# Attention and LoRA block on one core: FFN and next layer norm placed inside attention windows, split weights kept in memory, one distance table

## What is computed

```
x = x + attention(layernorm(x))
    q, k, v = x Wq^T, x Wk^T, x Wv^T ; q, k = rmsnorm(q) wq, rmsnorm(k) wk
    scores  = q k^T / sqrt(128) + slope[head] * (key position - query position), masked above the diagonal
    out     = softmax(scores) v ; y = out Wo^T
x = x + 2 * sum over experts h of (x_n A_h^T) B_h^T * 8 * softmax(x_n Wr^T + br)_h,   x_n = layernorm(x)
```

## Time and profile before

| | |
|---|---|
| Median of 3 runs | 2248.26 us (2247.36 to 2248.58) |
| The profiled execution, its own time | 2247.54 us |
| Span of the profile, first to last instruction | 2245.7 us |
| Busy: PE / DVE / ACT / POOL | 2168.2 / 1399.3 / 1185.8 / 912.5 us |
| Granted TensorE clock, mean | 0.993 of 2.4 GHz |
| DMA | 53.04 MB |

### The profile page before, as it was taken

The page is one execution under the profiler, slowest core; times in us unless marked ns, Lnnn a source line. Parts: engine busy times, 40 slices in busy tenths (PEclk is TensorE's granted clock), DMA queues, the critical chain, the costliest instruction groups (busy, mean ns, idle before and its releaser), DMA issues.

```text
span 2245.7 us, 33802 instructions
## 1 busy us (share of the span) xinstructions
PE 2168.2 (97%) x12540; PEld 1872.5 (83%) x12540; DVE 1399.3 (62%) x3492; ACT 1185.8 (53%) x3397; POOL 912.5 (41%) x912
## 2 busy tenths in 40 slices
PE   5999999999999999999869999999999999999997
PEld 5888888888888888888658888888888888888885
DVE  4666666566666666666656566665666666566666
ACT  3555555565555556555235555554555555455552
POOL 2444343444344444434124444434344344444441
PEclk9999999999999999999989999999999999999999
DMA  3001010010101001010120010100001010010001
GB/s 114 28 1 48 1 48 1 1 47 1 48 1 48 1 1 48 1 48 1 42 63 19 1 48 1 48 1 26 23 1 48 1 48 1 16 33 1 1 1 38
DMA packets 27907, 53.04 MB, mean 24 GB/s; under 512 B 3032, under 2 KB 3032, under 8 KB 27744
## 3 DMA queue, kind: packets, MB, share of 16 engines
q1 hardware_dynamic: 26112, 50.34, 7.0%
q10 hardware_dynamic: 1632, 0.55, 0.1%
HBM read 46.68 MB, written 4.19 MB: 23 GB/s over the span
## 4 chain that ended last, share of the span: by engine, by line
PE 93%; DVE 3%; ACT 1%; issue 1%; DMA 1%; POOL 1%; ACTq 0%
PE s_ps L863 25%; PE turn_ps L855 18%; PE o_ps L863 18%; PE q_ps L863 16%; PE y_ps L863 16%; DVE pT_lo L688 1%; DMA bias<-in_L_ffn_B 1%; ACT pT_hi L488 1%; DVE y L837 0%; ACT qn L531 0%; PE q_ps L1013 0%; DVE probs L716 0%; DVE stats L795 0%; DVE y L791 0%; POOL q_inv_t L583 0%
## 5 line engine op out<-in xcount | busy, mean ns | idle before, releaser
L612 POOL TENSOR_TENSOR probs<-probs,p_inv_t 128x896 f32<-128x896 f32 (+7 forms) x512 | 576.8, 1147 | 636.3 <-DVE p_inv_t L756 636.3
L488 ACT ACTIVATE pT_hi<-turn_ps 128x512 fp32r<-128x512 f32 x576 | 332.9, 600 | 485.6 <-PE turn_ps L855 483.6
L688 DVE TENSOR_TENSOR pT_lo<-turn_ps,pT_hi 128x512 fp32r<-128x512 f32 x576 | 383.0, 684 | 141.9 <-ACT pT_hi L488 138.6
L748 DVE CUSTOM_DVE_ANT_0 probs<-s_ps,bias 128x896 f32<-128x896 f32 (+7 forms) x512 | 381.3, 753 | 111.9 <-issue 110.4
L525 ACT ACTIVATE probs<-probs,neg_max 128x896 f32<-128x896 f32 (+7 forms) x512 | 396.1, 775 | 84.8 <-DVE neg_max L748 84.6
L855 PE MATMUL turn_ps<-ident,probs 128*128 128x128 f32 x2560 | 363.8, 278 | 23.8 <-POOL probs L612 9.5
L855 PEld LDWEIGHTS turn_ps<-ident,probs 128*128 128x128 f32 x2560 | 308.6, 143 | 77.0 <-POOL probs L612 15.4
L863 PE MATMUL s_ps<-kT_hi,qT_hi 128*128 128x512 f32 (+3 forms) x768 | 276.8, 360 | 0.3 <-DVE qT_lo L690 0.3
L863 PE MATMUL s_ps<-kT_hi,qT_lo 128*128 128x512 f32 (+3 forms) x768 | 262.8, 342 | 0.0
L863 PE MATMUL o_ps<-pT_hi,v_hi 128*128 128x512 f32 x576 | 249.4, 433 | 13.6 <-DVE pT_lo L688 13.2
L863 PE MATMUL s_ps<-kT_lo,qT_hi 128*128 128x512 f32 (+3 forms) x768 | 261.8, 341 | 0.0
(11 more groups left out here) (98 smaller groups left out, 3932.8 us busy)
## 6 DMA issues: line engine op xcount, KB each, us to landing
wq_raw<-in_L_attn_Wq SPq DMA_DIRECT2D x16, 1024.0 KB, 7.7
wo_raw<-in_L_attn_Wo SPq DMA_DIRECT2D x16, 1024.0 KB, 5.4
y<-in_L_attn_x SPq DMA_DIRECT2D x16, 256.0 KB, 3.2
wkv_raw<-in_L_attn_Wk SPq DMA_DIRECT2D x16, 256.0 KB, 2.8
wkv_raw<-in_L_attn_Wv SPq DMA_DIRECT2D x16, 256.0 KB, 3.0
out<-y SPq DMA_DIRECT2D x16, 256.0 KB, 2.0
bias<-in_L_ffn_A ACTq DMA_DIRECT2D x1, 256.0 KB
bias<-in_L_ffn_B ACTq DMA_DIRECT2D x1, 256.0 KB
```

Of the source, the lines that this page charges most:

```text
L488: nc.scalar.activation(target, source, ACT.Copy).then_inc(sems["hi_done"], 1)
L612: nc.gpsimd.tensor_tensor(row, row, p_inv_t[:, s % 2, h:h + 1].to_broadcast((P, L)), ALU.mult).then_inc(sems["p_ready"], 1)
L688: nc.vector.tensor_tensor(target, source, high.bitcast(F32), ALU.subtract).then_inc(sems["lo_done"], 1)
L748: nc.vector.tensor_tensor_reduce(out=probs[:, s % 2, h, 0:L], in0=s_ps[:, at_col:at_col + L], in1=bias[:, h, S - L:S], scale=-1.0, scalar= ...
```

## The change

The plans are written anew: PROLOGUE, GROUP_A (head groups of batch one, seven times), BOUNDARY (last group of batch one), FIRST_B, GROUP_B (six times), LAST. In place of counted offsets, each step has a number, and `after(engine, kind, ...)` waits for it. What is done otherwise:

- The layer norm of batch two, with its x turns, is in BOUNDARY. Its x is loaded into `wq_raw` and `wo_raw`, which no weight needs any more. The FFN of batch one runs in BOUNDARY (tiles 0 to 5) and FIRST_B (6 and 7), that of batch two in LAST. It has buffers of its own (two tiles deep), its logits go into a bank of the turn ring and are copied out by DVE, and its output uses `y_ps`.
- The FFN weights are loaded in BOUNDARY, into `wkv_raw`.
- After splitting a weight in batch one, SP writes both halves to DRAM (`keep_*`); in batch two it reads them back (`back_*`), and their turns and splits are gone.
- The bias tables are gone. q is divided by the head's slope through its norm, `score_max` adds the plain distance `rel` and scales by the slope.

```diff
-GROUP_PLAN = (
...
-    "inv_k turn.p.7.7 q_part.9.0 high.p.7.7 table.1 low.p.7.6 values.7.5 low.p.7.7 norm_k q_part.9.1 values.7.6 "
...
+BOUNDARY = (
...
+    "values.7.4 f_max.5 high.p.7.5 turn.p.7.6 f_exp.5 low.p.7.5 turn.p.7.7 high.p.7.6 f_inv.5 kv.3 f_gate.5 "
...
+    plans = {-1: read(PROLOGUE), NG - 1: read(BOUNDARY), NG: read(FIRST_B), LAST_W: read(LAST)}
+    group_a, group_b = read(GROUP_A), read(GROUP_B)
+    for w in range(LAST_W):
+        plans.setdefault(w, group_a if w < NG else group_b)
...
-        bias = sb("bias", [P, G, S])
+        f_x = sb("f_x", [P, 2, DM])
+        f_logits = sb("f_logits", [P, 2, P + NE])
...
+        def x_source(b, t):
+            if b == 0:
+                return y[:, t, :]
+            return wq_raw[:, t, :] if t < G else wo_raw[:, t - G, :]
...
+        wo_kept = nc.dram_tensor("wo_kept", [NG, 2, P, G * DM], F32).ap()
...
+            def keep_wo(w):
+                after(sp, "low", "wo", w, G - 1)
+                sp.dma_start(wo_kept[w, 0], woT_hi[:].rearrange("p c n -> p (c n)").bitcast(F32)).then_inc(wo_spilled, 16)
+                sp.dma_start(wo_kept[w, 1], woT_lo[:].rearrange("p c n -> p (c n)").bitcast(F32)).then_inc(wo_spilled, 16)
...
+            def back_wo(w):
+                g = w - NG
+                after(sp, "y", w - 1, NT - 1)
+                sp.wait_ge(wo_spilled, 32 * NG)
+                sp.dma_start(woT_hi[:].rearrange("p c n -> p (c n)").bitcast(F32), wo_kept[g, 0]).then_inc(wo_back, 16)
+                sp.dma_start(woT_lo[:].rearrange("p c n -> p (c n)").bitcast(F32), wo_kept[g, 1]).then_inc(wo_back, 16)
...
+            def square_q(w, n):
...
+                    last = nc.scalar.activation(qn[:, h, :], q_ps[:, h * HD:(h + 1) * HD], ACT.Square,
+                                                scale=float(slopes[gg % NG * G + h]), accum_out=q_sum[:, h:h + 1])
...
-                    def table(h):
...
-                        nc.gpsimd.tensor_tensor(bias[:, h, :], rel[:],
-                                                slope_row[:, bass.ds(g * G + h, 1)].to_broadcast((P, S)),
-                                                ALU.mult).then_inc(sems["bias_ready"], 1)
...
+            def score_max(w, s, h):
...
+                nc.vector.tensor_tensor_reduce(
+                    out=probs[:, s % 2, h, 0:L], in0=s_ps[:, at_col:at_col + L], in1=rel[:, S - L:S],
+                    scale=-float(slopes[w % NG * G + h]), scalar=BIG, op0=ALU.add, op1=ALU.min,
...
+                elif of == "logits":
+                    t, = which
+                    after(pe, "low", "f", ffn_batch(w), t)
+                    for c in range(C):
+                        last = nc.tensor.matmul(bank[:, 0:P + NE], f_x[:, t % 2, c * P:(c + 1) * P], arT[:, c, :],
```

More of the change, by code:

```diff
@@ L273, in piece, with follow @@
+    number, counted = {}, {}
+    for w in range(-1, LAST_W + 1):
+        for item in plans[w]:
+            if item[0] == "q" and item[2] < C - 1:
+                continue
+            counted[item[0]] = counted.get(item[0], 0) + 1
+            number[named(w, *item)] = counted[item[0]]
+    def follow(work):
+        for w in range(-1, LAST_W + 1):
+            for kind, *what in plans[w]:
+                if kind in work:
+                    work[kind](w, *what)
     def piece(s, j):
@@ L281, in scores_col @@
         return 512 * (h % 2) if L <= 512 else 512 - min(512, L - 256)
-    def follow(work, plan):
-        for kind, *what in plan:
-            if kind in work:
-                work[kind](*what)
     with ExitStack() as ctx:
@@ new lines, in load_wq, with load_wo @@
+            def load_wq(w, *first):
+                g = 0 if first else w + 2
+                if g < NG:
+                    if not first:
+                        after(sp, "turn", "wq", g - 1, C - 1)
+                    sp.dma_start(wq_raw[:], wq_v[g]).then_inc(wq_loaded, 16)
+            def load_wo(w, *first):
+                g = 0 if first else w + 1
+                if g < NG:
+                    if not first:
+                        after(sp, "turn", "wo", g - 1, G - 1)
+                    sp.dma_start(wo_raw[:], wo_v[g]).then_inc(wo_loaded, 16)
@@ new lines, in high, with exp @@
+                    nc.scalar.activation(target, bank, ACT.Copy, scale=scale).then_inc(sems["high"], 1)
+            def exp(w, s, h):
+                after(act, "max", w, s, h)
+                row = probs[:, s % 2, h, 0:(s + 1) * P]
+                nc.scalar.activation(row, row, ACT.Exp, bias=neg_max[:, s % 2, h:h + 1], scale=-1.0,
+                                     accum_out=p_sum[:, s % 2, h:h + 1]).then_inc(sems["exp"], 1)
+            def square_q(w, n):
+                gg, s = w + n // NT, n % NT
+                if w < 0 and s == 0:
+                    act.wait_ge(small_loaded, 48)
+                after(act, "q", gg, s, C - 1)
+                for h in range(G):
+                    last = nc.scalar.activation(qn[:, h, :], q_ps[:, h * HD:(h + 1) * HD], ACT.Square,
+                                                scale=float(slopes[gg % NG * G + h]), accum_out=q_sum[:, h:h + 1])
+                last.then_inc(sems["square_q"], 1)
@@ new lines, in square_k, with v_high @@
+            def square_k(w, i):
+                after(act, "kv", w + 1, i)
+                for t in range(2):
+                    last = nc.scalar.activation(k_norm[:, 2 * i + t, :], s_ps[:, 512 * (i % 2) + t * 2 * HD:][:, 0:HD],
+                                                ACT.Square, accum_out=k_sum[:, 2 * i + t:2 * i + t + 1])
+                last.then_inc(sems["square_k"], 1)
+            def v_high(w):
+                after(act, "copy_kv", w + 1, C - 1)
+                if w >= 0:
+                    after(act, "values", w, NT - 1, NT - 1)
+                nc.scalar.activation(v_hi[:], kv_raw[:, :, HD:2 * HD], ACT.Copy).then_inc(sems["v_high"], 1)
@@ new lines, in o_high, with f_exp @@
+            def o_high(w, s):
+                after(act, "values", w, s, s)
+                nc.scalar.activation(oT_hi[:].rearrange("p h n -> p (h n)"), o_ps[:], ACT.Copy).then_inc(sems["o_high"], 1)
+            def f_exp(w, t):
+                after(act, "f_max", ffn_batch(w), t)
+                nc.scalar.activation(f_weights[:, t % 2, :], f_biased[:, t % 2, :], ACT.Exp, bias=f_neg_max[:, t:t + 1],
+                                     scale=-1.0, accum_out=f_sum[:, t:t + 1]).then_inc(sems["f_exp"], 1)
@@ L565, in _, with sort_b @@
+            def sort_b(w):
+                act.wait_ge(b_loaded, 16)
+                after(act, "turn", "wr")
+                nc.scalar.activation(b_sorted.rearrange("p o h r -> p h o r"), b_raw, ACT.Copy).then_inc(sems["sort_b"], 1)
+            follow({"high": high, "exp": exp, "square_q": square_q, "square_k": square_k, "v_high": v_high,
+                    "o_high": o_high, "f_exp": f_exp, "sort_b": sort_b})
         @block.gpsimd
@@ new lines, in normalise @@
+            def normalise(w, s, h):
+                L = (s + 1) * P
+                if h % 2 == 0:
+                    after(pool, "invert", w, s, h // 2)
+                row = probs[:, s % 2, h, 0:L]
+                nc.gpsimd.tensor_tensor(row, row, p_inv[:, s % 2, h:h + 1].to_broadcast((P, L)),
+                                        ALU.mult).then_inc(sems["normalise"], 1)
+            follow({"inv_q": inv_q, "inv_k": inv_k, "x_rstd": x_rstd, "f_rstd": f_rstd, "normalise": normalise})
@@ new lines, in add_f @@
+            def add_f(w, t):
+                after(dve, "f_out", ffn_batch(w), t)
+                nc.vector.tensor_tensor(y[:, t, :], y_ps[:], y[:, t, :], ALU.add).then_inc(sems["add_f"], 1)
+            follow({"x_stats": x_stats, "x_moments": x_moments, "x_norm": x_norm, "low": low, "max": score_max, "invert": invert,
+                    "norm_q": norm_q, "copy_kv": copy_kv, "norm_k": norm_k, "v_low": v_low, "o_low": o_low, "add_y": add_y,
+                    "f_stats": f_stats, "f_moments": f_moments, "f_norm": f_norm, "f_max": f_max, "f_inv": f_inv,
+                    "f_gate": f_gate, "f_low": f_low, "add_f": add_f})
@@ L846, in _ @@
         @block.tensor
         def _(pe):
[L848 to L857 removed]
+            pe.wait_ge(ident_ready, 1)
@@ new lines, in scores @@
+            def scores(w, s, h):
+                L = (s + 1) * P
+                if h == 0:
+                    if s == 0:
+                        after(pe, "low", "k", w, 1)
+                    after(pe, "low", "q", w, s)
+                n = s * G + h - (1 if L > 512 else 2)
+                if n >= 0:
+                    after(pe, "max", w, n // G, n % G)
+                col = scores_col(s, h)
+                edge = L if L <= 512 else 512 - col
+                for c, width in ((0, edge), (edge, L - edge)):
+                    if width == 0:
+                        continue
+                    last = split_product(s_ps[:, col + c:col + c + width],
```

(52 more changed lines are left out.)

933 lines of the change are left out of this document (403 added, 530 removed), and 338 rows, old and new, of tables (BOUNDARY, FIRST_B, GROUP_A, GROUP_B).

## The result

The changed kernel takes **2194.25 us** (median of 3 runs, 2194.18 to 2194.96) against 2248.26: ratio 0.976, interval 0.974 to 0.978. The forecast was 2159, range 2138 to 2190. The direction was right; the gain was 54 us where 89 were forecast, and the time lies 4 us above the range. The profiled execution's span is 2193.1 us.

The account below looks back on a forecast made before the run. PE, 97% busy, was taken to bound the kernel. Savings of 11.3 + 3.5 + 42.7 + 22.0 + 0.3 + 9.3 = 89.1 us took 2247.54 to 2158.4, forecast as a median of 2159, range 2138 to 2190.

Parts of the forecast that it names:

- The reloads: Kept weight halves read back in batch two: landing in 8.3 to 10.8 us, 3.6 to 6 to spare, cost 0.
- about as much room: Wq's reload between q.7.3 and q.8.0 was said to have about the slack of woT's, 3.6 to 6 us.
- The waits for k: New PE stall at scores.0.0, each window's end, for kT_lo: 0.9 us in batch one, 1.9 in batch two.
- w7: Batch one's last window, taking the next layer norm and six FFN tiles: 150.1 against 192.81 us, so -42.7.
- PE's own work in a steady window is 131.76 less 1.49 = 130.3 us.: Middle windows: window time less the 1.49 us spot where a probability piece is turned and at once needed.
- Same operations, other order: Batch one's windows before its last: reordering itself given no cost, only one stall going and another coming.
- the small waits: PE's minor waits beside the one for k: 0.3 us allowed per middle window of batch two.
- w9 to w14: Batch two's middle windows, ten turns fewer, bare k stall: 128.1 against 131.77 us each, -22.0 for six.
- FFN tile of 1.95 ... logits 0.47 ... the logits' row is two tiles: PE's price per FFN tile: turn 0.44, logits 0.47, gate turn 0.16, output 0.88; six tiles 11.7 us.
- w0 to w6: Batch one's windows before its last: 1.49 stall goes, 0.9 k stall comes, net -0.5 us each, -3.5 together.
- Rival 1: FFN-laden windows don't fit DVE (2174 us), or norms held by GpSimd's normalises at 0.95 each (2179); chance 0.20 for both.
- w15 and the end: Last window with six FFN tiles 127.5 us, then a 12.7 us tail: 140.2 against 149.46, so -9.3.

Follow-up runs that it names:

- the two corrected kernels: Changed kernel with k turned ahead of y.7, plus kv.3 ahead of values.7.4: 2172.2 us; plus q 9.3 behind values.7.7 as well: 2166.2 us.
- the fastest kernel: Changed kernel with k turned ahead of y.7, kv.3 earlier, q 9.3 behind values.7.7, GpSimd's normalises held behind the FFN's gates, PE's start waits filled: 2161.1 us.

## Why the prediction was right and wrong

**Right.** *The reloads*: no product waits for kept weights in the changed kernel; the halves of Wo land 4.9 and 7.0 us after their issue, where I had 8.3 to 10.8.

```profile
woT_hi<-wo_kept SPq DMA_DIRECT2D x8, 1024.0 KB, 4.9
woT_lo<-wo_kept SPq DMA_DIRECT2D x8, 1024.0 KB, 7.0
```

The step "about as much room" for Wq holds only since q 8.0 was moved too: the run that turned Wo in batch one's order shows what it costs otherwise. The waits for k were sized right, 0.85 for 0.9 and 1.94 for 1.9. norm_k takes 1.23 in all 16 groups. *w7* is right in its total, 151.69 against 150.1, but in part by luck: its work was set 3.2 too low (1.0 and 2.2, below) and its waits 2.3 too high; 0.7 of the miss stays unexplained.

**Wrong: "PE's own work in a steady window is 131.76 less 1.49 = 130.3 us."** This is the step that failed: it carried 16 windows. The 1.49 from 327.88 to 329.37 is a stretch of the chain, that is, ACT and DVE at work on the high and low half; it is not time in which PE stood. Up to 328.57 PE ran six score products:

```profile
327.62 0.37 PE L863 MATMUL s_ps<-kT_hi,qT_hi 128*128 128x256 f32 x1
...
328.29 0.28 PE L863 MATMUL s_ps<-kT_hi,qT_lo 128*128 128x256 f32 x1
329.37 0.47 PE L863 MATMUL o_ps<-pT_hi,v_hi 128*128 128x512 f32 x1 [0.79 <-DVE pT_lo L688]
```

The wait is 0.8, and from start to start 0.96: the work was 130.8. The prediction had the right size in its own first paragraph, "PE idle for 0.8 us". Less their waits, the windows after are 131.33 and 126.87, 1.0 above the 130.3 and 125.9 of the forecast. Half of that 1.0 is the misread stall. The other half comes with the new order: "Same operations, other order" had been costed at nothing. What in the order makes it is open. It is not the number of changes from one kind of product to another: batch one has 138 runs of like products in a window against 130, but batch two has 125 and is as far above the forecast, and the two corrected kernels have 140 runs each and differ by 0.5 in their work. A first product behind a transpose takes 0.09 us longer up to the next, but starts 0.08 sooner behind the transpose, before and after alike.

**Wrong: the small waits.** The forecast had 0 beside the wait for k in batch one and 0.3 in batch two; they are 0.44 (y.7 for oT_lo) and 1.2. With the 1.0 of work this is 6 x 1.4 = 8.6 in w1 to w6 and 6 x 1.9 = 11.4 in w9 to w14, of the 8.5 and 14.4 missed.

**Missing: the clock.** There are two drops in w9 to w14 (3.1), and one each in the start and in w0 (1.3 and 1.6, by the run with the idle filled), 6 us together.

**Wrong: "FFN tile of 1.95 ... logits 0.47 ... the logits' row is two tiles".** The row with x8 is one tile: 128 such matmuls stand for 16 tiles in either kernel. From start to start a tile's logits take 0.84. The difference of 0.4 in 16 tiles is 6 us: 2.2 of w7, 0.8 of w8, the rest in w15 and the end. In w7 waits of 3.6, where 5.9 had been set, made up for it. A small slip beside it: for w0 to w6 the stall that goes (1.49) less the one that comes (0.9) is 0.6 a window, not 0.5.

**Rival 1's mechanism, not its place.** It put the lock on the norms at half a normalise each. Of the 24 norms in such windows seven took over 0.55 us (the longest 1.42), together 3.0 us more than alone, where the rival had 23. The gates met it, for up to a whole normalise; they had been costed at their durations from the tail of before, where GpSimd is idle. The Trainium skill ("SBUF — State Buffer", section "Who interferes with whom") has it that whichever of the two starts first has the ports for its whole instruction; the starts and ends of f_gates and low_gated beside the two normalises agree, and so does the run that keeps them apart. It gave back 3.6 us here, not the 20 of the rival.

**w15 and the end** miss by 6.0: 1.0 of work, about 2.4 of logits, an end of 14.4 for 12.7, and about 1 of waits. The end's 1.7 is the clock again, 0.78 there in the row above: the last tile's logits take 1.78 us where the tile's before took 1.09.

**Which cause is shown.** By experiment: the waits at the group's end (2194.3 to 2178.1, and to 2166.2 once their successors went too, the clock drops behind them included), the clock (5 us), the gates (3.6 in their windows, and 2.0 again in w7 of the fastest kernel). By rows alone: the misread stall, the logits. Left open: the half microsecond of work in each window, some 8 us in 16 windows. That w15 takes between 146.2 and 149.5 in kernels with the same order there goes with the clock: no drop ahead of the last tile in the windows of 146.2 and 146.7, one in those of 147.7, 147.9 and 148.5, two in the one of 149.5. Why a drop comes in one execution and not in another is open.

## What to carry to other kernels

Take a steady window's own work from a row of waits, start to start, not from a stretch of the chain, in which the bound engine may be busy with something else; an error of half a microsecond there is paid once per window. Where a change takes work off the bound engine, ask what that work was covering: four turns of Wo were worth 1.76 us and covered 0.9 of a wait. And compare windows, not totals: twice here a total matched a theory whose windows refuted it.
